# Score stacks of a whole pair in three buffers, projections three pairs ahead, and another order of the start, in an attention and expert kernel

## What is computed

```python
xl = _layer_norm(x, ln_l_g, ln_l_b)
xg = _layer_norm(x, ln_g_g, ln_g_b)
o = _mha(xl[:, 0:32], ...)           # "local": B = 32, so the 32 sequences attend over their first 32 tokens
local[:, 0:32] = o
glb = _mha(xg, xg, xg, ...)          # "global": each sequence over its 256 tokens, 16 heads of 8
x = _layernorm(x + local + glb)
# mixture of experts: a token goes to the expert of its largest logit, 8 experts, at most 1024 tokens each
expert_in = einsum('tec,th->ech', dispatch, tokens)
hidden = relu(einsum('ech,ehf->ecf', expert_in, W1) + b1)
expert_out = einsum('ecf,efh->ech', hidden, W2) + b2
x = _layernorm(x + gate * expert_out_of_each_token)
```

## Time and profile before

| | |
|---|---|
| median of 3 runs | 737.11 us (735.25 to 737.82) |
| the profiled execution | 735.65 us, its span 733.9 us |
| TensorE busy | 634.0 us (86%) |
| VectorE busy | 565.0 us (77%) |
| ScalarE busy | 490.5 us (67%) |
| GpSimd busy | 473.6 us (65%) |
| TensorE's granted clock, mean | 0.942 of full speed |
| read from and written to DRAM | 47.70 MB and 45.74 MB |
| the queue of SyncE (q1) | 85.54 MB, 138048 packets, 49.6% of the 16 DMA engines' time |

### The profile page before, as it was taken

The page is one execution under the profiler, slowest core; times in us unless marked ns, Lnnn a source line. Parts: engine busy times, 40 slices in busy tenths (PEclk is TensorE's granted clock), DMA queues, the critical chain, the costliest instruction groups (busy, mean ns, idle before and its releaser), DMA issues.

```text
span 733.9 us, 19237 instructions
## 1 busy us (share of the span) xinstructions
PE 634.0 (86%) x6502; PEld 357.8 (49%) x6502; DVE 565.0 (77%) x1716; ACT 490.5 (67%) x1108; POOL 473.6 (65%) x908
## 2 busy tenths in 40 slices
PE   0479689899999999999999999999999359999991
PEld 0335444444554445444544445445444227777771
DVE  5566597899999989999999899998894305666664
ACT  1426476787887988888888888888888224443430
POOL 4232334568778787787877877885666613666666
PEclk9858898999999999999999999999999669999996
DMA  5575589997556566565566765655631022333410
GB/s 120 141 171 141 120 206 177 234 208 172 154 119 162 154 131 169 156 128 152 106 167 157 140 169 141 118 156 108 145 76 36 24 64 75 104 106 94 123 52 33
DMA packets 144001, 95.53 MB, mean 130 GB/s; under 512 B 12052, under 2 KB 136173, under 8 KB 143904
## 3 DMA queue, kind: packets, MB, share of 16 engines
q1 hardware_dynamic: 138048, 85.54, 49.6%
q0 software_dynamic: 4096, 7.81, 3.8%
q10 hardware_dynamic: 1760, 0.96, 0.6%
HBM read 47.70 MB, written 45.74 MB: 127 GB/s over the span
## 4 chain that ended last, share of the span: by engine, by line
PE 44%; DVE 16%; POOL 13%; issue 10%; DMA 9%; SPq 5%; ACT 2%; POOLq 0%; ACTq 0%; DVEq 0%
DVE mx L942 9%; PE ps_o L557 8%; PE ps_a L1388 6%; PE ps_b L530 5%; DMA qs<-mT 4%; PE ps_b L1382 4%; PE ps_a L512 3%; DMA ks<-k_stack 3%; POOL row L1213 3%; POOL routed L1241 2%; PE ps_f L468 2%; PE ps_f L478 2%; PE ps_f L473 2%; POOL out L1502 2%; POOL rstd L1202 2%
## 5 line engine op out<-in xcount | busy, mean ns | idle before, releaser
L942 DVE TENSOR_REDUCE mx<-ps_a 128x2 f32<-128x512 f32 (+1 forms) x576 | 359.6, 649 | 45.0 <-PE ps_a L512 42.7
L764 ACT ACTIVATE prob<-ps_b 128x512 f32<-128x512 f32 (+1 forms) x576 | 299.6, 573 | 74.0 <-PE ps_b L530 72.6
L530 PE MATMUL ps_b<-qs,ks 59*128 59x256 bf16 (+1 forms) x1152 | 191.3, 270 | 12.7 <-DMA qs<-mT 6.2
L512 PE MATMUL ps_a<-ks,qs 56*128 56x256 bf16 (+1 forms) x1152 | 188.7, 274 | 14.2 <-DMA ks<-k_stack 12.2
L557 PE MATMUL ps_o<-prob,vp 128*32 128x256 f32 (+1 forms) x2304 | 172.4, 384 | 0.4 <-ACT prob L764 0.4
L530 PEld LDWEIGHTS ps_b<-qs,ks 59*128 59x128 bf16 x1152 | 80.5, 95 | 101.9 <-ACT prob L764 48.7
L512 PEld LDWEIGHTS ps_a<-ks,qs 56*128 56x128 bf16 x1152 | 75.7, 96 | 27.8 <-DMA ks<-k_stack 13.0
L1241 POOL DMA_INDIRECT routed<-row,slot x64 | 67.2, 1050 | 31.7 <-issue 31.7
L1502 POOL DMA_INDIRECT out<-res,dest x64 | 64.8, 1012 | 34.2 <-DVE res L1477 19.0
L557 PEld LDWEIGHTS ps_o<-prob,vp 128*32 128x32 f32 x2304 | 49.7, 109 | 58.0 <-issue 49.8
L1176 POOL CAST mpart<-mx 128x16 bf16<-128x16 f32 x72 | 14.2, 197 | 86.5 <-DVE mx L942 74.1
(11 more groups left out here) (130 smaller groups left out, 1042.8 us busy)
## 6 DMA issues: line engine op xcount, KB each, us to landing
qs<-q_stack SPq DMA_DIRECT2D x72, 192.0 KB
ks<-k_stack SPq DMA_DIRECT2D x72, 192.0 KB
q_stack<-part SPq DMA_DIRECT2D x18, 384.0 KB
k_stack<-part SPq DMA_DIRECT2D x18, 384.0 KB
q_stack<-part SPq DMA_DIRECT2D x18, 256.0 KB
k_stack<-part SPq DMA_DIRECT2D x18, 256.0 KB
routed<-empty SPq DMA_DIRECT2D x8, 520.0 KB, 7.7
rows_sb<-routed SPq DMA_DIRECT2D x16, 260.0 KB, 3.6
```

What stands on the lines that cost most here:

```text
L512: ins = nc.tensor.matmul(ps_a[:, n % 3, qt * S:qt * S + keys.stop - keys.start], qs[half, b, hp, qt * P:(qt + 1) * P], ks[half, b, hp, key ...
L530: ins = nc.tensor.matmul(ps_b[:, 1 - e, kt * n:(kt + 1) * n], ks[half, u % 3, hp, kt * P:(kt + 1) * P], qs[half, u % 3, hp, queries], star ...
L764: nc.scalar.activation(prob[:, hp, half * n:(half + 1) * n], ps_b[:, half, 0:n], ACT.Exp).then_inc(exp_done, 1)
L942: nc.vector.reduce_max(mx[:, u % 2, :, col], ps_a[:, n % 3].rearrange("p (t k) -> p t k", t=2)[:, :, 0:k], axis=AX).then_inc(max_done, 1)
```

## The change

The parts of it:

- `qs` and `ks` hold three buffers of a whole pair (`[P, 3, 8, 512]`), and `load_stacks(p)` fetches a pair in four DMAs of 393,216 bytes, in rows of 512 tokens (1 KB). It is issued at odd u, behind `place_max(u, 1)`, for pair (u + 3) // 2, so that units u + 3 and u + 4 are fetched together.
- AHEAD = 3: three pairs are projected and stored before the loop, and the loop projects pair u // 2 + 3. `vp` has 8 buffers in place of 6. The third pair's work that GpSimd had in the loop (`third_part`) is done by VectorE before the loop.
- The maxima's rows now lie right under the stack (rows 48 to 50) and the mask's under them (51 to 58). Global units use 48 and 51 rows and so leave the mask out; `nomask` is gone. Local units use 59 rows in both passes.
- The memset of `ks` is gone. `place_rows` puts three rows of minus ones into `ks` (all three pair buffers) and three rows of zeros into `qs` (the two local pair buffers), by four DMAs: 2 x 73,728 and 2 x 49,152 bytes. `place_mask` fills the two local pair buffers, by four DMAs of 131,072 bytes (before: four of 98,304).
- VectorE casts the mask after the statistics of pairs 0 and 1, and normalizes pair 0 before it waits for the x of pair 1. ScalarE's queue fetches the weights before the masks. The prologue's v goes to `ps_o`.
- `res` of the experts lies in `vp`.

```diff
@@ constants
-AHEAD = 2
+AHEAD = 3
-MASKROW = STACK
+MAXROW = STACK
+MASKROW = MAXROW + 3
 NBLK = S // LW
-MAXROW = MASKROW + NBLK
-KMAX = MAXROW
-KEXP = MAXROW + 3
+KLOCAL = MASKROW + NBLK
@@ buffers
-    qs = sb("qs", [P, 3, NH // 2, S], BF16)
-    ks = sb("ks", [P, 3, NH // 2, S], BF16)
-    vp = sb("vp", [P, 6, 2, NH, 32])
+    qs = sb("qs", [P, 3, NH // 2, PAIR], BF16)
+    ks = sb("ks", [P, 3, NH // 2, PAIR], BF16)
+    vp = sb("vp", [P, 2 * AHEAD + 2, 2, NH, 32])
@@ sync
+        def place_rows():
+            sp.wait_ge(rows_set, 2)
+            for e in range(2):
+                at = HALF * e + MAXROW
+                sp.dma_start(ks[at:at + 3].rearrange("p b g n -> p (b g) n"),
+                             minus_ones[:].unsqueeze(1).to_broadcast([3, 3 * NH // 2, PAIR])).then_inc(rows_placed, 16)
+                sp.dma_start(qs[at:at + 3, 0:LPAIR].rearrange("p b g n -> p (b g) n"),
+                             no_max[:].unsqueeze(1).to_broadcast([3, LPAIR * NH // 2, PAIR])).then_inc(rows_placed, 16)
...
-        def load_stack(u):
-
-            b, h, p = u % 3, u % 2, u // 2
-            wait(sp, scores, 16 * (u - 2))
+        def load_stacks(p):
+
+            b = p % 3
+            wait(sp, scores, 16 * (2 * p - 4))
             sp.wait_ge(stack_stored[p % 2], 96 * (p // 2 + 1))
...
             for dst, stack in ((qs, q_stack), (ks, k_stack)):
-                src = stack[p, :, :, h * S:(h + 1) * S].rearrange("(g e d) t n -> e (d t) g n", e=2, d=DH)
+                src = stack[p].rearrange("(g e d) t n -> e (d t) g n", e=2, d=DH)
                 for e in range(2):
                     sp.dma_start(dst[HALF * e:HALF * e + STACK, b], src[e]).then_inc(stack_loaded[b], 16)
@@ sync, step(u)
-            if u % 2 == 1 and there(u + 2):
-                load_stack(u + 2)
             if there(u):
                 place_max(u, 1)
-            if u % 2 == 0 and there(u + 2):
-                load_stack(u + 2)
+            if u % 2 == 1 and (u + 3) // 2 < NPAIR:
+                load_stacks((u + 3) // 2)
...
-            if u % 2 == 1 and (u + 1) // 2 + 1 < NPAIR:
-                store_stacks((u + 1) // 2 + 1)
+            if second_pair(u) is not None:
+                store_stacks(second_pair(u))
@@ sync, before the loop
-        for p in range(AHEAD + 1):
+        for p in range(AHEAD):
             load_x(p)
+        place_rows()
         place_mask()
+        load_x(AHEAD)
         load_x(AHEAD + 1)
         store_stacks(0)
-        load_stack(0)
-        load_stack(1)
+        load_stacks(0)
         store_stacks(1)
+        store_stacks(2)
+        load_stacks(1)
         place_max(0, 0)
@@ vector, before the loop
-        nc.vector.memset(ks[:].bitcast(F32), TWO_MINUS_ONES).then_inc(stacks_cleared, 1)
-        nc.vector.memset(nomask[:].bitcast(U32), 0).then_inc(stacks_cleared, 1)
-        dve.wait_ge(mask_loaded, 32)
-        nc.vector.tensor_copy(block_qb[:], block_q[:]).then_inc(mask_cast, 1)
-        nc.vector.tensor_copy(block_kb[:], block_k[:]).then_inc(mask_cast, 1)
+        nc.vector.memset(minus_ones[:].bitcast(F32), TWO_MINUS_ONES).then_inc(rows_set, 1)
+        nc.vector.memset(no_max[:].bitcast(U32), 0).then_inc(rows_set, 1)
+        input_stats(0, (0, 1, 2, 3))
+        input_variance(0)
...
+        normalize_first(0)
         input_stats(1, (0, 1, 2, 3))
-        normalize_first(0)
         input_variance(1)
         nc.vector.tensor_copy(c["ident_bf"][:], c["ident"][:])
+        dve.wait_ge(mask_loaded, 32)
+        nc.vector.tensor_copy(block_qb[:], block_q[:].unsqueeze(1).to_broadcast([NBLK, 2, S])).then_inc(mask_cast, 1)
+        nc.vector.tensor_copy(block_kb[:], block_k[:].unsqueeze(1).to_broadcast([NBLK, 2, S])).then_inc(mask_cast, 1)
         normalize_first(1)
```

More of the change, by code:

```diff
@@ L282, in layer @@
     tail = experts(nc, ctx, c, expert_weights, routed, out, scattered, o1_stored,
-                   dict(hT=prob, ps_h=[ps_b[:, 0], ps_b[:, 1], ps_a[:, 2], ps_f[:]], ps_y=ps_a, ps_x=ps_o))
+                   dict(hT=prob, res=vp, ps_h=[ps_b[:, 0], ps_b[:, 1], ps_a[:, 2], ps_f[:]], ps_y=ps_a, ps_x=ps_o))
     block = ctx.enter_context(nc.Block(no_gpsimd_drain=True))
@@ L379, in place_max @@
                 at = HALF * e + MAXROW
-                sp.dma_start(qs[at:at + 3, u % 3, 4 * half:4 * half + 4, :],
+                sp.dma_start(qs[at:at + 3, (u // 2) % 3, 4 * half:4 * half + 4, (u % 2) * S:(u % 2 + 1) * S],
                              mT[12 * e:12 * e + 12, half, :]).then_inc(max_rows[half], 16)
@@ L496, in max_pass @@
         def max_pass(u, hp, e, qt):
-            b = u % 3
-            if hp == 0 and e == 0 and qt == 0:
-                extra = 0 if u < LU else 32
-                pe.wait_ge(stack_loaded[b], 64 * (u // 3 + 1) + extra)
+            p, first = u // 2, (u % 2) * S
+            b = p % 3
+            if first == 0 and hp == 0 and e == 0 and qt == 0:
+                pe.wait_ge(stack_loaded[b], 64 * (p // 3 + 1))
                 if u == 0:
                     pe.wait_ge(mask_placed, 64)
+                    pe.wait_ge(rows_placed, 64)
             n = 16 * u + 2 * hp + e
@@ L506, in max_pass @@
                 wait(pe, max_done, n - 2)
-                if n == 2:
-                    pe.wait_ge(v_placed, AHEAD)
-            keys = slice(qt * P, (qt + 1) * P) if is_local(u) else slice(0, S)
-            half = slice(HALF * e, HALF * e + KMAX)
+            queries = slice(first + qt * P, first + (qt + 1) * P)
+            keys = queries if is_local(u) else slice(first, first + S)
+            half = slice(HALF * e, HALF * e + (KLOCAL if is_local(u) else STACK))
             ins = nc.tensor.matmul(ps_a[:, n % 3, qt * S:qt * S + keys.stop - keys.start],
-                                   qs[half, b, hp, qt * P:(qt + 1) * P],
+                                   qs[half, b, hp, queries],
                                    ks[half, b, hp, keys], start=True, stop=True)
@@ L527, in exp_pass @@
             n = P if is_local(u) else S
-            queries = slice(kt * P, (kt + 1) * P) if is_local(u) else slice(0, S)
-            half = slice(HALF * e, HALF * e + KEXP)
+            b, first = (u // 2) % 3, (u % 2) * S
+            keys = slice(first + kt * P, first + (kt + 1) * P)
+            queries = keys if is_local(u) else slice(first, first + S)
+            half = slice(HALF * e, HALF * e + (KLOCAL if is_local(u) else MAXROW + 3))
             ins = nc.tensor.matmul(ps_b[:, 1 - e, kt * n:(kt + 1) * n],
-                                   ks[half, u % 3, hp, kt * P:(kt + 1) * P],
-                                   qs[half, u % 3, hp, queries], start=True, stop=True)
+                                   ks[half, b, hp, keys],
+                                   qs[half, b, hp, queries], start=True, stop=True)
             if kt == 1:
@@ L922, in normalize_first @@
             dve.wait_ge(frstd_ready, p + 1)
+            wait(dve, xT_ready, p - 1)
             for t in range(4):
@@ L1111, in _ @@
         take_rest_k(0)
+        input_stats(2, (0, 1, 2, 3))
+        input_variance(2)
         third_first(0)
+        normalize_first(2)
         nc.vector.memset(c["ones_bf"][:], 1.0)
@@ L1128, in _ @@
         third_first(1)
-        for p in (AHEAD, AHEAD + 1):
-            input_stats(p, (0, 1, 2, 3))
-            input_variance(p)
+        input_stats(AHEAD, (0, 1, 2, 3))
+        input_variance(AHEAD)
+        take_rest_q(2)
+        take_rest_k(2)
+        third_first(2)
+        input_stats(AHEAD + 1, (0, 1, 2, 3))
+        input_variance(AHEAD + 1)
         dve.wait_ge(bv_projected, 1)
@@ L1267, in _ @@
         pool.wait_ge(pow_set, 1)
-        input_deviation(0)
-        input_deviation(1)
-        input_deviation(2)
-        pool.wait_ge(xh_ready, 2)
-        normalize_input(2)
+        for p in range(AHEAD + 1):
+            input_deviation(p)
+        pool.wait_ge(xh_ready, AHEAD)
+        normalize_input(AHEAD)
         split_max(0, 0)
@@ L1311, in experts @@
     rstd = sb("e_rstd", [P, 2, CT])
-    res = sb("res", [P, 4, CT, D])
+    res = lent["res"][:].rearrange("p c k u w -> p (c k u w)")[:, 0:4 * CT * D].rearrange("p (k t d) -> p k t d", k=4, t=CT)
     dest = sb("dest", [P, 4, CT], U32)
```

41 lines of the change are left out of this document (17 added, 24 removed).

## The result

The changed kernel takes **845.13 us** (median, 841.46 to 848.83), the kernel before 736.42 beside it: ratio **1.147**, 95% interval 1.143 to 1.151. The prediction said 763 with a range of 733 to 774: slower was right, the size was a quarter of what came. The profiled execution has a span of 840.9 us.

What follows compares the result with a forecast made beforehand. TensorE and VectorE bound the loop, one DMA queue the start. 5.4 + 12.7 + 13 + 5 - 7.0 - 2.7 = +26.4 on 735.65 gave 762.1, and 1.5 for the median made 763 us, range 733 to 774.

Steps and rivals of the forecast that it cites:

- Bytes or packets: Loads: cost goes by bytes per partition, not packets, so 1 KB rows keep 178 GB/s and a pair takes 8.8 us.
- the 5.6 us that a fit gave for a pair: Loads: an estimate from the notes' fit of one DMA, 2.0 us plus bytes over 436 GB/s.
- Step 1: Start up to the store of pair 0: larger placements make it land at about 37 us, +5.4.
- Step 2: From that store to the first scores: loads and stores in one queue take 28.3 us, not 15.6, +12.7.
- Step 3, the entry to unit 2: Early loop: maxima behind the pair's load come late, 4.0 us lost, part of +13 for the early units.
- Step 3, the steady loop: Maxima behind the load come 0.85 us late for each of 12 pairs, half absorbed: +5 (0 to +12).
- Step 4: Savings: unit 4's load wait and the low clock after it, -7.0; one pair fewer projected in the loop, -2.7.
- The rivals: Three cases: loads and placements by packet, 729 (0.12); loads only, 737 (0.08); small placements pass large transfers, 737 (0.08).

Runs made afterwards that it cites:

- c5: b1 with the rows for maxima set by memsets of `ks` and `qs` in place of `place_rows`; 739.11 us, ratio 1.006 to the kernel before.
- a4: a1 with `store_stacks(2)` moved behind the load of pair 1 and the first placement; 823.29 us, ratio 1.119 to the kernel before.
- c4: b1 with `place_max(0, 0)` ahead of the loads of pair 1 in the prologue; 738.54 us, ratio 1.0037 to the kernel before.
- a1: The changed kernel with `store_o1` issued ahead of `load_stacks` in each step; 827.45 us, ratio 1.127 to the kernel before.
- b1: The changed kernel with one unit's half of a pair loaded in each loop step, not whole pairs; 748.92 us, ratio 1.010 to the kernel before.
- b4: The kernel before with one edit: VectorE normalizes pair 0 ahead of the statistics of pair 1; 740.71 against 742.33 us, ratio 0.998.

## Why the prediction was right and wrong

- **Bytes or packets**: right in the main. Loads of 1 KB rows moved 176 to 179 GB/s in the start, stores 397; the 5.6 us that a fit gave for a pair did not come. The reason given was wrong: the rates of the earlier trace rows are not one rate per partition (178 GB/s over 96 partitions, 375 over 128 and 47 over 8 are 1.9, 2.9 and 5.9 each). The 8.8 us came from the nearest row and did not need it. The Trainium skill ("SBUF — State Buffer", Door 1: The DMA port swizzle) gives 196 GB/s for 8 of 16 ports, and the trace stays a little under it. In the loop the rate was lower, 146 to 155 in the windows shown, which the forecast did not have.
- **Step 1, +5.4**: right in size (37.87 for 37), and partly by luck, as errors cancel: the placements had left the queue at 26.7 and not at 29.4, the x of pairs 3 and 4 held it for 4.2 us and not 1.5, and the store took 6.9 to land and not 5.4. Of the placements, the 3-partition rows cost 3.6 (c5).
- **Step 2, +12.7**: right in size (65.12 for 65). Its 4.2 for the store of pair 2 was not: without it scores came 0.6 earlier (a4), since the load of pair 1 waits for the store of pair 1 to land all the same. The order of placement and load was 5.9 of it (c4).
- **Step 3, the entry to unit 2**: the mechanism right, a wait of 7.7 us in place of 4.0. From the first scores to the store of step 7 the lag grew from 17.9 to 28.3 us.
- **Step 3, the steady loop, 0.85 us a pair and +5 in all: this step failed.** Measured are 6.3 us a pair, and 67.7 us from the store of step 7 to that of step 29. Three things in it were wrong. *First*, only `place_max` was looked at behind the load. `store_o1` stands there too, and its single buffer carries the delay to ScalarE and TensorE; in the kernel before it stood behind 4.4 us of data at most. *Second*, "out at 211.5, through at 222.6" was too early: in a1 the load goes out at 319.80, 2.0 us behind the placement of 317.78, its data take 10 to 11 us and not 8.8, and the next placement lands at 333.7, 15.9 behind 317.78 where the forecast had 12.6 (210.04 to 222.6). Needed 11.7 behind it, it is 4.3 late, not 0.85. *Third*, half was taken as absorbed. In a loop in which TensorE and VectorE are busy 27.9 and 27.7 of 29.5 us hardly anything can be: in a1 a placement 4.3 late goes with a pair 4.8 longer. The lower clock adds some 0.8 to 1.7 us to an idle time (the estimates above).
- **Step 4, -9.7**: b1 agrees in size. It begins scores 16.9 us later than the kernel before and ends some 7 later (0.96%), so 9.8 came back. The trace of b4, which is the kernel before but for its first scores and ran with b1, gives the same: b1 is 18.7 us behind it at the first scores, 13.7 at the store of step 29 and 9.2 at the end. How much of it is the load of unit 4 and how much the end was not taken apart. In the change itself nothing of it shows: the lag grows by another 11 us from the store of step 29 to the end.
- **The rivals** all lay on the faster side. None took a slow loop: that the steady state could be worse than the start was missing from the range.

## What to carry to other kernels

A transfer costs not only its bytes but the longest gap that it opens for every small transfer behind it; before merging two loads into one, list all that shares the queue until it has drained, with the time when each is next needed, and cut the load to less than the shortest of these gaps. In this kernel loads that land in 5 us cost nothing between placements 5 to 10 us apart, loads of 10 us cost 2 to 6 us a pair. When a wait is removed and little is gained, look for the next one under it, at the same place: here a late output store hid late maxima. Where two engines are full, count each idle time whole, and add what the clock takes behind it.
